# Attention on one core: the product with the inverse sums on GpSimd, row maxima six tiles ahead, and layer 2's maximum products on two groups of 64 rows

## Chip, core and metric

One Trainium2 chip, one of its cores. The time is that of the whole program on the device, in microseconds (us). The kernel before is measured in three runs, and one further execution is profiled.

## What is computed

The input is an image of 32 x 32 positions with 384 channels, that is 1024 tokens. Three residual blocks follow each other:

```
x = x + conv_attention(groupnorm(x))            # layer 1: 12 heads of 32, relative position terms
t = t + attention(layernorm(t))                 # layer 2: 12 heads of 32
t = t + experts(layernorm(t))                   # 8 experts, the best 2 of each token

per head:  attn = softmax(q k^T * scale (+ rel_h + rel_w in layer 1));  out = attn v
```

The change concerns the 12 heads of both attention layers.

## The kernel before, in words

Every engine has its own instruction stream, written out by hand, and semaphores tie them together. Each stream runs layer 1 (L = 0 in the code) and layer 2 (L = 1) with the same code. A layer first makes q, k and v, splits q and k into a rounded part and a rest, and writes them to DRAM by head; then come 12 heads, numbered 0 to 11; then the projection and the next normalisation. Heads 0, 1, 10 and 11 are written out, heads 2 to 9 are two turns of a loop of four heads.

A head is worked through in eight tiles of 128 keys, s = 0 to 7 (`head` in each engine's block):

- TensorE makes the transposed scores of tile s (`scores`, L618, and L620 for the position terms in layer 1), 128 keys by 1024 queries in two banks. Behind them it makes the *maximum products* (`max_scores`, L603): one tile of 128 queries against all 1024 keys, in two halves of 512 keys, from the head's own copies qm and km. After each odd s it makes the output products of two earlier tiles (`out_product`, L628). Only VectorE's maximum of each query is wanted from the maximum products.
- VectorE takes the maximum over each half of 512 (`maximum`, L891). The halves rotate through three PSUM banks (`RING`), so a product waits until VectorE has read the bank that was used three halves before. When the eight tiles of a head are done, the maxima are transposed (`turn_max`, L608), copied by ScalarE (`turned_max`), stored to DRAM and loaded as row 96 of qa (`place_max`), so that the scores of that head come out with the maximum subtracted.
- `AHEAD` says how many tiles the maximum products run ahead of the scores: with 5, tile s of head h makes tile s + 5 of head h + 1, or, from s = 3, tile s - 3 of head h + 2. The list `MAXIMA` holds this as (heads ahead, tile).
- ScalarE takes the exponential of each tile into one of six buffers of prob (L1074). GpSimd adds up tiles 0 to 5 in layer 1 and 0 to 4 in layer 2 (`add_tiles`, L514 for the first, L518 for the others, one 128x1024 addition each), and TensorE sums the remaining tiles and this sum over the keys (`sums`).
- Output products and sums of head h - 1 are finished at s = 1 of head h. ScalarE copies them to vsb (`keep_output`, L1100). At s = 3 to 6 VectorE inverts the sums in four pieces (`invert_sums`, L901) and after s = 6 multiplies (`output`, L906, 128x256), which counts o_ok up.
- SyncE issues the DMAs in one queue. One turn of its loop, for head h, is: `load_m(h + 1)` (qm and km, L379 and L380), `load_a(h)` (qa, ka, qb), in layer 2 three stores of zeros (L449), and `store(h - 2)`, which waits for o_ok and then issues four DMAs (L314). `load_m(h + 1)` waits for the end of the maximum products of head h - 1, whose buffers it overwrites, and stands behind the stores of head h - 3. TensorE waits for it (ld_m) before tile 0 of the maximum products of head h + 1.

In layer 1 qm and km have 96 rows in use: three parts of q and k of 32 rows. In layer 2 the product has 32 rows that count; rows 32 to 95 of qm are set to zero between the layers (L933), so that the same 96-row product can be used.

## Time and profile before

| | us |
|---|---|
| median of three runs | 1006.41 |
| lowest, highest | 1001.41, 1008.95 |
| the profiled execution | 1002.1 |
| its span in the trace | 1000.3 |
| layer 1's heads 2 to 9 | about 159 to 302 |
| layer 2's heads 2 to 9 | about 449 to 585 |
| experts | about 650 to the end |

The trace holds one execution. A row of a time line gives the start of a group of instructions, the time from the start of the first to the end of the last, the engine, the line of the kernel, the operation with output and inputs, the shapes, and in brackets how long the engine stood idle before it and who released it. A matmul's end is modelled and reaches into the next one, so the distance between starts is what counts on TensorE (PE). DVE is VectorE, ACT ScalarE, POOL GpSimd, SP SyncE; SPq is SyncE's queue of DMA issues.

### The profile page before, as it was taken

The numbers are of one execution on the slowest core, as the hardware profiler recorded it, in microseconds if no ns is written. First come the engines' busy times: TensorE is split into PE (matmuls) and PEld (weight loads), VectorE is DVE, ScalarE is ACT, GpSimd is POOL, SyncE is SP. The second block draws the span as 40 slices with busy tenths as digits, with TensorE's granted clock in tenths as the row PEclk, the third lists the DMA queues.
The fourth block names the chain that finished last, engine by engine and source line by source line (L and its number), as shares of the span: only waits on it lengthen the run. The fifth ranks groups of instructions, "written<-read, shape, count | busy, mean of one in ns | idle before, by whom it ended". The sixth has DMA issues, their size and how long they took to land.

```text
span 1000.3 us, 17750 instructions
## 1 busy us (share of the span) xinstructions
PE 879.1 (88%) x6029; PEld 641.9 (64%) x6030; DVE 526.9 (53%) x883; ACT 328.3 (33%) x582; POOL 457.2 (46%) x360
## 2 busy tenths in 40 slices
PE   4969899999998899999898978616999999999991
PEld 3457466566665444555454534516999999999991
DVE  4334767676776444878788772722233333233224
ACT  0212144554545222445454544201222322322230
POOL 0000076676778200346464665558076177077303
PEclk9989699999999999999999989957999999999996
DMA  9564723534424019335464571351356455455214
GB/s 291 109 147 150 271 76 87 130 104 110 127 84 154 11 32 231 92 84 176 127 206 126 195 241 37 125 185 49 115 179 219 145 174 197 167 181 176 87 32 141
DMA packets 74367, 139.23 MB, mean 139 GB/s; under 512 B 11000, under 2 KB 49080, under 8 KB 74320
## 3 DMA queue, kind: packets, MB, share of 16 engines
q1 hardware_dynamic: 62720, 120.42, 39.3%
q10 hardware_dynamic: 9552, 11.93, 3.6%
q0 software_dynamic: 2048, 6.29, 2.0%
q8 instruction: 24, 0.39, 0.2%
q14 instruction: 23, 0.19, 0.1%
HBM read 91.39 MB, written 43.55 MB: 135 GB/s over the span
## 4 chain that ended last, share of the span: by engine, by line
PE 43%; issue 8%; DVE 8%; POOL 6%; DMA 3%; ACT 1%; DVEq 0%; SPq 0%; POOLq 0%; ACTq 0%
PE ps L796 14%; PE ps L807 11%; DVE mhalf L891 4%; PE ps L628 4%; PE ps L585 3%; PE ps L603 3%; POOL qf L518 3%; PE ps L727 2%; PE ps L618 2%; POOL xs L547 1%; POOL gy L556 1%; PE ps L683 1%; DVE rec L901 1%; PE ps L778 1%; ACT prob L1074 1%
## 5 line engine op out<-in xcount | busy, mean ns | idle before, releaser
L891 DVE TENSOR_REDUCE mhalf<-ps 128x1 f32<-128x512 f32 x384 | 242.0, 679 | 95.6 <-PE ps L603 94.1
L1074 ACT ACTIVATE prob<-ps 128x1024 f32<-128x1024 f32 x192 | 190.5, 1026 | 186.7 <-PE ps L628 110.0
L518 POOL TENSOR_TENSOR qf<-qf,prob 128x1024 f32<-128x1024 f32 x84 | 206.1, 2453 | 18.2 <-POOL qf L518 8.1
L796 PE MATMUL ps<-xT,w 128*128 128x128 f32 x1440 | 166.8, 278 | 1.6 <-ACT xT L1146 1.4
L796 PEld LDWEIGHTS ps<-xT,w 128*128 128x128 f32 x1440 | 166.1, 194 | 2.1 <-issue 2.1
L603 PE MATMUL ps<-km,qm 96*128 96x512 f32 x384 | 145.3, 445 | 20.1 <-DVE mhalf L891 15.3
L618 PE MATMUL ps<-qa,ka 97*128 97x512 f32 x384 | 147.4, 426 | 8.6 <-DMA qa<-row 8.2
L1163 ACT ACTIVATE h_f<-ps,b1c 128x128 f32<-128x128 f32 x240 | 68.4, 368 | 215.6 <-PE ps L796 161.0
L603 PEld LDWEIGHTS ps<-km,qm 96*128 96x128 f32 x384 | 74.1, 194 | 71.5 <-DVE mhalf L891 51.9
L514 POOL TENSOR_TENSOR qf<-prob 128x1024 f32<-128x1024 f32 x24 | 57.1, 2379 | 134.7 <-ACT prob L1074 134.7
L628 PE MATMUL ps<-prob,va 128*32 128x256 f32 x1536 | 109.8, 393 | 0.0
L1018 DVE CAST h_hi<-h_f 128x512 fp32r<-128x512 f32 x60 | 33.6, 560 | 144.6 <-ACT h_f L1163 142.4
L499 POOL TENSOR_SCALAR w_hi<-w_raw 128x384 fp32r<-128x384 f32 x96 | 54.6, 569 | 112.1 <-DMA w_raw<-in_w 105.4
L501 POOL TENSOR_TENSOR w_lo<-w_raw,w_hi 128x384 fp32r<-128x384 f32 x96 | 101.2, 1054 | 8.0
L618 PEld LDWEIGHTS ps<-qa,ka 97*128 97x128 f32 x384 | 69.4, 192 | 50.7 <-ACT prob L1074 23.6
L528 POOL COPY va<-vf 128x256 f32 (+1 forms) x24 | 9.5, 396 | 187.7 <-DVE vf L877 102.4
L807 PE MATMUL ps<-w_hi,h_hi 128*128 128x384 f32 x240 | 82.0, 342 | 0.0
L807 PE MATMUL ps<-w_lo,h_hi 128*128 128x384 f32 x240 | 80.4, 335 | 0.0
L807 PE MATMUL ps<-w_hi,h_lo 128*128 128x384 f32 x240 | 80.4, 335 | 0.0
L620 PE MATMUL ps<-qb,eb 128*128 128x512 f32 x192 | 76.9, 400 | 0.0
L628 PEld LDWEIGHTS ps<-prob,va 128*32 128x32 f32 x1536 | 40.9, 111 | 47.3 <-issue 29.2
L585 PE MATMUL ps<-xnT,wqkv 128*128 128x512 f32 x144 | 63.6, 604 | 3.1 <-DVE xnT L852 3.1
(130 smaller groups left out, 874.5 us busy)
## 6 DMA issues: line engine op xcount, KB each, us to landing
w<-in_w SPq DMA_DIRECT2D x24, 768.0 KB, 7.4
w_raw<-in_w SPq DMA_DIRECT2D x24, 768.0 KB, 12.0
heads<-parts SPq DMA_DIRECT2D x56, 256.0 KB, 4.7
qa<-heads SPq DMA_DIRECT2D x24, 256.0 KB, 3.7
ka<-heads SPq DMA_DIRECT2D x24, 256.0 KB, 3.9
qb<-heads SPq DMA_DIRECT2D x12, 512.0 KB, 5.1
xs<-zero SPq DMA_DIRECT2D x8, 768.0 KB, 4.9
qm<-heads SPq DMA_DIRECT2D x12, 384.0 KB, 3.7
```

Source lines behind the costliest of these rows:

```text
L501: pool.tensor_tensor(w2_lo[b][:, c, :], w2_raw[b][:, c, :], f(w2_hi[b][:, c, :]), ALU.subtract).then_inc(w2_ok[b], 1)
L518: pool.tensor_tensor(acc[b], acc[b], prob[:, n % NP, :], ALU.add).then_inc(a_ok[L], 1)
L585: last = mm(ps[:, 2 * (u % 2) + half, :], wqkv[:, k, col * P:(col + 1) * P], xnT[:, k, half * HALF:(half + 1) * HALF], start=(k == 0), sto ...
L603: mm(max_bank(qt, half), qm[b][0:96, qt * P:(qt + 1) * P], km[b][0:96, half * HALF:(half + 1) * HALF], start=True, stop=True).then_inc(sm_ ...
L618: last = mm(out, ka[b][0:97, s * P:(s + 1) * P], qa[b][0:97, cols], start=True, stop=(L == 1))
L620: last = mm(out, eb[:, s * P:(s + 1) * P], qb[b][:, cols], start=False, stop=True)
L628: last = mm(ps[HD * r:HD * (r + 1), 6, half * QUARTER:(half + 1) * QUARTER], lhs, src[:, r * QUARTER:(r + 1) * QUARTER], start=start, stop ...
L796: last = mm(ps[:, g, c % HG * P:(c % HG + 1) * P], w1[b][:, k, c * P:(c + 1) * P], xT[:, k, :], start=(k == 0), stop=(k == KT - 1))
L807: last = mm(ps[:, 6, 0:C], h[:, c, :], w[:, c, :], start=(c == 0 and n == 0), stop=(c == HC - 1 and n == 2))
L891: v.tensor_reduce(mhalf[:, b, qt, half:half + 1], max_bank(qt, half), AX.X, ALU.max).then_inc(mx_ok[L], 1)
L1074: act.activation(prob[:, s % NP, :], ps[:, 2 + 2 * (s % 2):4 + 2 * (s % 2), :].rearrange("p a b -> p (a b)"), ACT.Exp).then_inc(p_ok[L], 1)
L1163: last = act.activation(h_f[:, c, :], ps[:, g, c % HG * P:(c % HG + 1) * P], ACT.Relu, bias=b1c[b][:, c:c + 1])
```

## The change

The product of the outputs with the inverse sums moves from VectorE to GpSimd, behind the last addition of the head after. `AHEAD` is 6 instead of 5. In layer 2 the first half of the keys is multiplied on rows 0 to 63 of the array and the second half on rows 64 to 127: qm and km grow to 128 rows, q's rounded part is loaded a second time into rows 64 to 95 of qm and the second half of k's into the same rows of km, and rows 96 to 127 are set to zero at the very start of VectorE's stream. The zeroing between the layers shrinks to rows 32 to 63.

```diff
-AHEAD = 5
+AHEAD = 6
-MAXIMA_FIRST = [[(1, 5)], [(1, 6)], [(1, 7)], [(2, 0)], [(2, 1)], [(2, 2)], [(2, 3)], [(2, 4)]]
+MAXIMA_FIRST = [[(1, 5), (1, 6)], [(1, 7)], [(2, 0)], [(2, 1)], [(2, 2)], [(2, 3)], [(2, 4)], [(2, 5)]]
-        qm = [put(f"qm{i}", [96, N], F32R) for i in range(2)]
-        km = [put(f"km{i}", [96, N], F32R) for i in range(2)]
+        qm = [put(f"qm{i}", [P, N], F32R) for i in range(2)]
+        km = [put(f"km{i}", [P, N], F32R) for i in range(2)]
@@ sync, load_m
                     sp.dma_start(f(km[b][0:HD, :]), rows(h, "K_HI")).then_inc(ld_m[L][b], 16)
+                    if L == 1:
+                        sp.dma_start(f(qm[b][64:96, :]), rows(h, "Q_HI")).then_inc(ld_m[L][b], 16)
+                        sp.dma_start(f(km[b][64:96, HALF:N]), rows(h, "K_HI")[:, HALF:N]).then_inc(ld_m[L][b], 16)
@@ gpsimd
-                def add_tiles(h, b, last=False):
+                def output(h, b):
+                    pool.wait_ge(o_rc[L], 4 * (h + 1))
+                    wait(pool, st_o[L][b], 32 * (h - b))
+                    pool.sem_inc(pool_in, 1)
+                    pool.tensor_tensor(osb[b][:], vsb[:, 0, :], rec[:], ALU.mult).then_inc(o_ok[L], 1)
+
+                def add_tiles(h, b, first=False, last=False):
                     for n in range(1, ADDS[L] + 1):
...
+                        if n == ADDS[L] and not first:
+                            output(h - 1, 1 - b)
+                    if last:
+                        output(h, b)
@@ tensor
-                n_m, n_a = (2, 5) if L == 0 else (2, 4)
+                n_m, n_a = (2, 5) if L == 0 else (4, 4)
...
-                        mm(max_bank(qt, half), qm[b][0:96, qt * P:(qt + 1) * P],
-                           km[b][0:96, half * HALF:(half + 1) * HALF], start=True, stop=True).then_inc(sm_ok[L], 1)
+                        rows = slice(0, 96) if L == 0 else slice(64 * half, 64 * half + 64)
+                        mm(max_bank(qt, half), qm[b][rows, qt * P:(qt + 1) * P],
+                           km[b][rows, half * HALF:(half + 1) * HALF], start=True, stop=True).then_inc(sm_ok[L], 1)
...
-                                pe.wait_ge(wide_ok, 4)
+                                pe.wait_ge(wide_ok, 6)
@@ vector, at its start
                 v.memset(f(ka[i][96:104, :]), 1.0)
+                for wide in (qm, km):
+                    v.memset(f(wide[i][96:P, :]), 0.0).then_inc(wide_ok, 1)
@@ vector, in the heads
-                def output(h, b):
-                    wait(v, st_o[L][b], 32 * (h - b))
-                    v.wait_ge(o_rc[L], 4 * (h + 1))
-                    v.tensor_tensor(osb[b][:], vsb[:, 0, :], rec[:], ALU.mult).then_inc(o_ok[L], 1)
...
-                        if s == 6 and not first:
-                            output(h - 1, 1 - b)
...
-                        for rows in (slice(32, 64), slice(64, 96)):
-                            v.memset(f(qm[i][rows, :]), 0.0).then_inc(wide_ok, 1)
+                        v.memset(f(qm[i][32:64, :]), 0.0).then_inc(wide_ok, 1)
...
-                output(NH - 1, 1)
```

The lines of the changed kernel are some steps further down: L511 is the product on GpSimd, L523 and L527 the additions, L617 the maximum products, L622 the transposition, L632 and L634 the scores, L642 the output products.

On GpSimd, in the loop of layer 1, the last addition of one head and what follows it. Before (qf holds the running sum, va the values, prob the exponentials):

```order
L518 TENSOR_TENSOR qf<-qf,prob 128x1024
L508 ISA
L514 TENSOR_TENSOR qf<-prob 128x1024
L284 ISA
L528 ISA
L528 COPY va_67<-vf 128x256
```

and now:

```order
L527 TENSOR_TENSOR qf<-qf,prob 128x1024
L508 REGISTER_ALU
L284 REGISTER_ALU
L511 TENSOR_TENSOR osb_72<-vsb,rec 128x256
L517 ISA
L523 TENSOR_TENSOR qf<-prob 128x1024
```

The product to osb has come between the last addition of a head and the first of the next.

On TensorE, in the loop of layer 1, tiles 2 and 3 of a head before (km_63 and qm_61 belong to the next head, km_64 and qm_62 to the one after it; qa, ka, qb are of the head itself):

```order
L618 MATMUL ps<-qa_58,ka_60 128x512
L620 MATMUL ps<-qb_66,eb 128x512
L602 REGISTER_ALU
L603 MATMUL ps<-km_63,qm_61 128x512
L602 REGISTER_ALU
L603 MATMUL ps<-km_63,qm_61 128x512
L284 REGISTER_ALU
L618 MATMUL ps<-qa_58,ka_60 128x512
L620 MATMUL ps<-qb_66,eb 128x512
L618 MATMUL ps<-qa_58,ka_60 128x512
L620 MATMUL ps<-qb_66,eb 128x512
```

and tile 2 now:

```order
L632 MATMUL ps<-qa_58,ka_60 128x512
L634 MATMUL ps<-qb_66,eb 128x512
L632 MATMUL ps<-qa_58,ka_60 128x512
L634 MATMUL ps<-qb_66,eb 128x512
L284 ISA
L617 MATMUL ps<-km_64,qm_62 128x512 x2
L622 MATMUL ps<-ident,mcol 8x128
L284 REGISTER_ALU
```

The first maximum products of the second head ahead stood behind tile 3 and stand behind tile 2, and the transposition directly behind them.

In SyncE's queue, in the loop of layer 2, the last of the four stores of an output and the loads behind it. Before:

```order
L314 DMA xnT<-osb_71 32x256
L284 REGISTER_ALU
L379 ISA
L379 DMA qm_61<-heads 32x1024
L380 ISA
L380 DMA km_63<-heads 32x1024
L284 REGISTER_ALU
```

and now:

```order
L314 DMA xnT<-osb_72 32x256
L284 REGISTER_ALU
L379 ISA
L379 DMA qm_62<-heads 32x1024
L380 ISA
L380 DMA km_64<-heads 32x1024
L382 DMA qm_62<-heads 32x1024
L383 ISA
L383 DMA km_64<-heads 32x512
L284 REGISTER_ALU
```

Two loads have been added; their place behind the stores is the same.

## Rows read from the trace of the kernel before

**Rows 1.** Busy time of each engine in a stretch of each layer: PE, PEld, DVE, ACT, POOL, clock.

```profile
250.00:300.00 50.00, 50.00 (x387) 31.99 (x389) 37.71 (x66) 24.04 (x27) 36.65 (x18) 1.00 0.38 106
550.00:600.00 50.00, 41.60 (x357) 22.02 (x353) 39.33 (x53) 24.65 (x30) 32.62 (x15) 0.94 0.65 217
```

**Rows 2.** TensorE's maximum products in the time line, layer 1.

```profile
198.29 0.73 PE L603 MATMUL ps<-km,qm 96*128 96x512 f32 x2 [0.26 <-DVE mhalf L891]
...
249.69 0.63 PE L603 MATMUL ps<-km,qm 96*128 96x512 f32 x2
...
251.09 0.88 PE L603 MATMUL ps<-km,qm 96*128 96x512 f32 x2
```

**Rows 3.** VectorE's products with the inverse sums in the time line, layer 1.

```profile
188.42 2.20 DVE L906 TENSOR_TENSOR osb<-vsb,rec 128x256 f32<-128x256 f32 x1
...
242.60 0.55 DVE L906 TENSOR_TENSOR osb<-vsb,rec 128x256 f32<-128x256 f32 x1
```

**Rows 4.** GpSimd's additions in the time line, layer 1.

```profile
159.46 2.39 POOL L514 TENSOR_TENSOR qf<-prob 128x1024 f32<-128x1024 f32 x1 [4.52 <-ACT prob L1074]
...
231.96 2.37 POOL L514 TENSOR_TENSOR qf<-prob 128x1024 f32<-128x1024 f32 x1 [4.25 <-ACT prob L1074]
...
243.05 2.38 POOL L518 TENSOR_TENSOR qf<-qf,prob 128x1024 f32<-128x1024 f32 x1 [0.18 <-ACT prob L1074]
249.69 2.39 POOL L514 TENSOR_TENSOR qf<-prob 128x1024 f32<-128x1024 f32 x1 [4.27 <-ACT prob L1074]
...
302.41 2.38 POOL L514 TENSOR_TENSOR qf<-prob 128x1024 f32<-128x1024 f32 x1 [4.19 <-ACT prob L1074]
```

**Rows 5.** TensorE in the time line, layer 2.

```profile
528.80 0.50 PE L603 MATMUL ps<-km,qm 96*128 96x512 f32 x1 [1.31 <-DVE mhalf L891]
...
533.28 0.62 PE L603 MATMUL ps<-km,qm 96*128 96x512 f32 x2
...
534.46 1.10 PE L603 MATMUL ps<-km,qm 96*128 96x512 f32 x2
...
540.71 0.63 PE L618 MATMUL ps<-qa,ka 97*128 97x512 f32 x2
541.17 0.76 PE L603 MATMUL ps<-km,qm 96*128 96x512 f32 x2
541.87 1.07 PE L628 MATMUL ps<-prob,va 128*32 128x256 f32 x16
```

**Rows 6.** VectorE's product with the inverse sums in the time line, layer 2.

```profile
525.69 2.45 DVE L906 TENSOR_TENSOR osb<-vsb,rec 128x256 f32<-128x256 f32 x1
```

**Rows 7.** SyncE's queue in the time line, layer 2: the loads of qm and km.

```profile
531.28 0.36 SPq L379 DMA_DIRECT2D qm<-heads  x1
531.84 0.35 SPq L380 DMA_DIRECT2D km<-heads  x1
```

**Rows 8.** GpSimd's additions in the time line, layer 2.

```profile
430.52 2.37 POOL L514 TENSOR_TENSOR qf<-prob 128x1024 f32<-128x1024 f32 x1 [4.85 <-ACT prob L1074]
...
448.63 2.37 POOL L514 TENSOR_TENSOR qf<-prob 128x1024 f32<-128x1024 f32 x1 [7.40 <-ACT prob L1074]
...
533.76 2.37 POOL L514 TENSOR_TENSOR qf<-prob 128x1024 f32<-128x1024 f32 x1 [5.90 <-ACT prob L1074]
...
542.19 2.38 POOL L518 TENSOR_TENSOR qf<-qf,prob 128x1024 f32<-128x1024 f32 x1 [0.18 <-POOL qf L518]
...
585.32 2.40 POOL L514 TENSOR_TENSOR qf<-prob 128x1024 f32<-128x1024 f32 x1 [5.91 <-ACT prob L1074]
```

**Rows 9.** Busy time and granted clock in a stretch of layer 2, columns as above.

```profile
442.00:450.00 8.00, 7.75 (x52) 3.96 (x52) 4.33 (x8) 3.75 (x5) 1.37 (x1) 0.79 0.49 139
```

**Rows 10.** TensorE at the start of layer 2's head 11, in the time line.

```profile
597.65 0.77 PE L618 MATMUL ps<-qa,ka 97*128 97x512 f32 x1 [5.49 <-DMA qa<-row]
```

**Rows 11.** VectorE at the program's start, in the time line.

```profile
2.74 0.91 DVE L824 MEMSET ka<- 8x1024 f32 x1 [0.16 <-issue]
...
4.23 1.36 DVE L838 BATCH_NORM_STATS2 stat<-xnT 128x6 f32<-128x512 f32 x2
```

More of the change, by code:

```diff
@@ L530, in _ @@
                 take_v(0, 0)
-                add_tiles(0, 0)
+                add_tiles(0, 0, first=True)
                 add_tiles(1, 1)
```

## The prediction

> **What bounds the kernel now.** I read four views in this order: the busy time by stretch, the time line of TensorE through one head of each layer, that of VectorE, SyncE's queue and GpSimd over the same stretch, and the sequence of heads seen from GpSimd's first addition. Call R the moment in a head at which TensorE comes to the maximum products of tile 2, M a pair of such products, S the scores of a tile.
>
> In layer 1 TensorE is busy for all of 50 us; in layer 2 for 41.6 of 50 [rows 1]. Layer 1's heads take (302.41 - 249.69) / 3 = 17.57 us where nothing disturbs them, and (302.41 - 159.46) / 8 = 17.87 over the loop [rows 4]. Layer 2's take (585.32 - 448.63) / 8 = 17.09 [rows 8]. So layer 1 has nothing to give on other engines, and layer 2 has some: in one head TensorE waits 1.31 us for VectorE, because VectorE's 256-column product took 2.45 us there [rows 5, 6]. In layer 1, where it fell into a gap of GpSimd's, the same product took 0.55 [rows 3].
>
> One loop counts above all. The loads of a head's qm and km stand in SyncE's queue behind the stores of an output made a head before, and M of the second head ahead waits for them. In layer 1 an output ends at 188.42 + 2.20 = 190.62 and M starts at 198.29, 7.67 later; another ends at 243.15, and M starts on time at 251.09, 7.94 later [rows 2, 3]. In layer 2 the output ends at 525.69 + 2.45 = 528.14, the loads of qm and km are issued at 531.28 and 531.84, and M starts at 534.46 [rows 5 to 7]; VectorE frees its bank at the same moment, so the row alone doesn't say which of the two it waited for. Load and slot meet within a few tenths in both layers: there is no slack for what comes later.
>
> **The change, part by part.**
>
> *The product on GpSimd.* It now stands behind the last addition. In layer 1 the additions run from 231.96 to 243.05 + 2.38 = 245.43, 13.47 us [rows 4]. The product has a quarter of the columns of an addition: 2.38 / 4 = 0.6, with a start gap of 0.2 some 0.8. It ends at R + 14.3 (the first addition starts at R: both at 249.69 [rows 2, 4]), where VectorE was done at 243.15, so 3.1 us later. In layer 2 the additions take 542.19 - 533.76 + 2.38 = 10.8 and start 0.48 behind R (533.28) [rows 5, 8]; with 0.87 the output ends at R + 12.15.
>
> *Maxima six ahead.* The first M of the second head ahead moves from tile 3 to tile 2: its slot is 251.09 - 249.69 = 1.4 us earlier in layer 1, 534.46 - 533.28 = 1.2 in layer 2.
>
> *Two more loads in layer 2.* They are issued 0.56 apart as the two before (531.28, 531.84 [rows 7]); with the gap to the next issue 0.6 each, 1.2 more before the last lands.
>
> *The loop, layer 1.* Output at R + 14.3, landing and weight load 7.8 later: M is possible at R + 22.1. TensorE comes to it at R + 17.3 (the 17.57 without the 0.25 by which the second M at 251.09 is slow, 0.88 against 0.63 [rows 2]). A wait X moves R of the next head but not the additions of its own head, so two waits in a row add up to 22.1 - 17.3 = 4.8, and a head takes (22.1 + 17.3) / 2 = 19.7. A first wait of 4.8 also holds the third and fourth additions (scores of tile 3 come late) by some 1.8 once. Eight heads (loads 4 to 11 stand behind a store): 8 x 19.7 + 2.4 (the first wait above the mean) = 160, against 142.95. **Plus 17.0 us.**
>
> *Layer 2's pairs.* If the two products run at once, each of the 8 pairs saves one start distance, 0.46 / 2 = 0.23 (S to M, 540.71 to 541.17 [rows 5]): 1.86 a head. But M now stands between products of 97 rows. The one change of array shape that the trace shows, M to the output products (541.17 to 541.87), costs 0.70 - 0.46 = 0.24 beyond the pair [rows 5]. A head gets 12 more changes of shape (three per two tiles). Bounds for one: nothing and 0.24, together 0 to 2.9 us a head; below nothing it can't be, since nothing is removed. I take 0.1, 1.2 a head, somewhat below the middle: the 0.24 also holds the weight loads of four column groups, which a change of row groups does not have.
>
> The Trainium skill speaks against this part: its page "TensorEngine Tiling (Array Packing)", section "Key Properties", says that changing the tiling mode, not only the tile, drains TensorE. The trace agrees for column groups, by the 0.24 above; no row here shows it for row groups. By the rule the upper bound holds, and the pairs would cost 1.0 a head instead of saving 0.7.
>
> *TensorE's own head in layer 2*, free of waits: 16.7 less 1.31, less 0.34 (1.10 against 0.76 for the pair at 534.46) and some 0.7 in smaller slips is 14.4 [rows 5]. Then - 1.86 + 1.2 + 0.45 (VectorE's 16 maxima and 4 reciprocals still fill their tiles) = 14.2. VectorE loses 2.4 a head and no longer binds.
>
> *The loop, layer 2.* M possible at R + 12.15 + 6.3 (528.14 to 534.46) + 1.2 = R + 19.7; period (19.7 + 14.2) / 2 = 17.0, eight times, with 2.8 for the first wait: 138.8 against 136.69. **Plus 2.1.** So what the pairs and the freed VectorE bring is spent waiting for the loads.
>
> *Head 1 of layer 2* has no load behind a store ahead of it. It took 448.63 - 430.5 = 18.1, part of it at a granted clock of 0.79 on average [rows 8, 9]; now 14.2 and a little: **minus 3.5.** *Head 10 to 11*: TensorE waits 5.49 for the row of maxima [rows 10]; the transposition now stands a tile and a pair of output products earlier, 1.9 us: **minus 1.9.**
>
> *The clock.* In 442 to 450 the granted clock averages 0.79, its lower level of 1.2 GHz for part of the stretch, after such a wait [rows 9]; the same view shows it in three of the loop's eight heads. Waits of 3 us a head should bring more of it. A fall costs some 1.5, half of which the load's lateness hides: **plus 2** (bounds 0 and 6).
>
> *Start.* Four more memsets of 32x1024 run ahead of the first statistics, which begin the moment VectorE is free. A memset of 1024 columns takes 0.91 and a start gap of 0.16 (2.74), 1.07 together, and nothing stands between the last memset and the statistics at 4.23 [rows 11]: four are **plus 4.3**, less only if x lands after 4.23. Two memsets less between the layers lie beside TensorE's head 10 and bring nothing.
>
> *Ends of the layers.* The last product waits for reciprocals on another engine and takes 0.6 instead of 0.43: 0.5 each, and 0.8 once in layer 1, where GpSimd's additions are the end: **plus 1.8.**
>
> **Sum:** 4.3 + 17.0 + 1.8 - 3.5 + 2.1 - 1.9 + 2 = 21.8. The profiled execution took 1002.1 (span 1000.3), so 1023.9, say **1024 us**. That execution lies 4.3 below the median of the three runs (1006.41); against that median it would be 1.8% slower. About 1% is what a measurement of this kernel can tell from no change.
>
> **The rivals.**
>
> *A, forecast:* M waits for the load in both layers. For it: load and slot already meet. Against it: no row of layer 1 shows a wait of this size, only its beginning.
>
> *B, the loads keep up, faster.* The place is the same M. It decides at the point where the last load lands before the slot, that is, if from R to landing is under 17.3 in layer 1 and 14.2 in layer 2 instead of 22.1 and 19.7. Then layer 1 gives 8 x 0.57 = 4.6, layer 2 8 x 2.9 = 23.1, head 1 3.5, head 10 1.9, against 6.1 for start and ends: 1002.1 - 27.0 = 975. For it: layer 2's real waits of 1.31. Against it: the 7.67 and 6.32 measured between an output and its M.
>
> *C, changes of shape cost the upper bound.* TensorE's head in layer 2 is 15.9, the period 17.8: 8 x 17.8 + 1.9 for the first wait is plus 7.6 instead of 2.1; head 1 gives 1.9; the clock falls in every head, plus 6: 1002.1 + 4.3 + 17.0 + 1.8 + 7.6 - 1.9 - 1.9 + 6 = 1035. (This is also what the skill's rule on tiling modes comes to here.)
>
> *D, the pairs are free and the clock holds.* TensorE's head in layer 2 is 14.4 - 1.8 = 12.6, the period 16.15, with 3.6 for the first wait 132.8, minus 3.9; head 1 minus 5.1: 1002.1 + 4.3 + 17.0 + 1.8 - 3.9 - 5.1 - 1.9 = 1014, within 1% of the median.
>
> *E, the pairs don't overlap* (one starts behind the other): 1.86 back on TensorE, of which the loop shows half, 7.4 in eight heads, and 1.9 in head 1: 1033. It has its chance inside A and C.
>
> **How the numbers follow.** A 0.60, C 0.15, D 0.16, B 0.09. The range reaches from below D (1015, less if x lands late and hides the memsets: 4.3, and if layer 1's waits are 0.5 shorter each: 4) to C: 1006 to 1038. Faster by over 1% is most of B, 0.08; within 1% is D and a rest, 0.17; slower 0.75.
>
> **What would show it.** In the profile after, TensorE's largest wait is M for km or qm, 2 to 5 us in heads 2 to 9 of both layers, and GpSimd's first additions of layer 1 follow each other by 19.7 (17.57 before); the output ends 0.8 behind the last addition; SyncE's stores wait for GpSimd. The two products of a layer 2 pair start within a few ns of each other; S behind them starts 0.1 later than before. The first matmul of TensorE moves from 9.35 us by 4.3. The forecast is wrong if M starts without waiting at tile 2, if layer 2's period is under 16, or if the first statistics don't move.

## The result, and the profile after

The changed kernel takes 1067.69 us (median of four runs, 1059.92 to 1075.65), the kernel before, on the same chip, 1004.78 (1001.41 to 1008.95). The ratio is 1.0625, 95% interval 1.0524 to 1.0725: slower by 6%. The prediction said 1024, range 1006 to 1038. The direction and the place were right, the size was 44 us short. The profiled execution took 1059.9, its span is 1058.1 against 1000.3, and the mean granted clock of TensorE 0.917 against 0.945.

In this part R is the start of GpSimd's first addition in a head (L523, before L514). The prediction's R, the moment at which TensorE comes to the maximum products of tile 2, lies a few tenths beside it; where a forecast counts from that moment, I count from it too and say so. The 24 first additions divide the span:

| stretch | before | after | difference | forecast |
|---|---|---|---|---|
| to R of head 0, layer 1 | 123.7 | 129.8 | +6.1 | +4.3 |
| heads 0 and 1 | 35.7 | 39.8 | +4.1 | 0 |
| heads 2 to 9 | 143.0 | 162.5 | +19.5 | +17.0 |
| head 10 | 16.1 | 16.8 | +0.7 | 0 |
| R of head 11 to R of head 0, layer 2 | 96.4 | 100.8 | +4.4 | +1.3 |
| head 0 | 15.6 | 18.4 | +2.8 | 0 |
| head 1 | 18.1 | 16.8 | -1.3 | -3.5 |
| heads 2 to 9 | 136.7 | 158.0 | +21.3 | +2.1 |
| head 10 | 18.3 | 15.8 | -2.5 | -1.9 |
| from R of head 11 to the end | 396.6 | 399.3 | +2.7 | +0.5 |
| clock, in no one place | | | | +2 |

The list of waits of the changed kernel has at the place of the forecast (engine, output and line waited for, releaser, then us in all, times, longest):

```profile
PE ps L617 <- DMA km<-heads: 32.5, 19, 2.9
POOL osb L511 <- DVE rec L917: 22.6, 9, 4.5
```

Before, the first of these was 2.2 us in 4 waits, and the second did not exist. The busy time by stretch, in the columns of [rows 1]: two of the same stretches, then the eight heads of either loop.

```profile
250.00:300.00 50.00, 44.82 (x321) 27.18 (x314) 27.05 (x47) 21.79 (x27) 33.39 (x18) 0.93 0.41 116
550.00:600.00 50.00, 47.07 (x337) 20.79 (x337) 32.69 (x57) 22.40 (x25) 29.24 (x17) 0.86 0.49 157
170.00:332.00 162.00, 147.73 (x1096) 91.86 (x1097) 96.08 (x168) 70.10 (x80) 103.39 (x56) 0.96 0.34 95
485.00:643.00 158.00, 142.49 (x1034) 64.21 (x1035) 96.00 (x168) 69.48 (x81) 84.60 (x48) 0.86 0.48 150
```

TensorE, never idle in 250 to 300 before, is now idle for 5.2 us of it. In layer 2 it looks busier than before (47.07 against 41.60), but at a clock of 0.86: the same products last longer. Read without its clock, the busy share would have said that TensorE waits less there than before.

One turn of the loop in layer 1, GpSimd and then TensorE, answers to [rows 2 to 4]:

```profile
188.42 2.34 POOL L523 TENSOR_TENSOR qf<-prob 128x1024 f32<-128x1024 f32 x1 [4.67 <-ACT prob L1081]
...
202.20 0.73 POOL L511 TENSOR_TENSOR osb<-vsb,rec 128x256 f32<-128x256 f32 x1
208.94 2.34 POOL L523 TENSOR_TENSOR qf<-prob 128x1024 f32<-128x1024 f32 x1 [6.01 <-ACT prob L1081]
```

```profile
188.18 0.39 PE L634 MATMUL ps<-qb,eb 128*128 128x512 f32 x1
191.28 0.73 PE L617 MATMUL ps<-km,qm 96*128 96x512 f32 x2 [2.71 <-DMA km<-heads]
...
211.16 0.72 PE L617 MATMUL ps<-km,qm 96*128 96x512 f32 x2 [2.07 <-DMA km<-heads]
```

TensorE comes to the maximum products of tile 2 at 191.28 - 2.71 = 188.57. The output ends at 202.93, 14.4 later (forecast 14.3), and the M that needs the load behind it starts at 211.16, after a wait of 2.07: 22.6 later (forecast 22.1).

The same turn in layer 2, to be read against [rows 5, 7, 8]: TensorE, then GpSimd, then SyncE's queue.

```profile
527.45 0.61 PE L617 MATMUL ps<-km,qm 64*128 64x512 f32 x2 [1.80 <-DMA km<-heads]
...
548.69 0.50 PE L617 MATMUL ps<-km,qm 64*128 64x512 f32 x2 [1.75 <-DMA km<-heads]
...
563.83 0.73 PE L632 MATMUL ps<-qa,ka 97*128 97x512 f32 x2
566.68 0.49 PE L617 MATMUL ps<-km,qm 64*128 64x512 f32 x2 [2.12 <-DMA km<-heads]
```

```profile
540.89 0.73 POOL L511 TENSOR_TENSOR osb<-vsb,rec 128x256 f32<-128x256 f32 x1 [3.80 <-DVE rec L917]
547.25 2.35 POOL L523 TENSOR_TENSOR qf<-prob 128x1024 f32<-128x1024 f32 x1 [5.63 <-ACT prob L1081]
...
558.51 0.73 POOL L511 TENSOR_TENSOR osb<-vsb,rec 128x256 f32<-128x256 f32 x1 [0.49 <-DVE rec L917]
564.94 2.35 POOL L523 TENSOR_TENSOR qf<-prob 128x1024 f32<-128x1024 f32 x1 [5.70 <-ACT prob L1081]
```

```profile
559.38 2.60 SPq L314 DMA_DIRECT2D xnT<-osb  x4
562.79 0.37 SPq L379 DMA_DIRECT2D qm<-heads  x1
563.37 0.35 SPq L380 DMA_DIRECT2D km<-heads  x1
563.81 0.37 SPq L382 DMA_DIRECT2D qm<-heads  x1
564.36 0.32 SPq L383 DMA_DIRECT2D km<-heads  x1
```

The chain can be followed in them. TensorE comes to the maximum products of tile 2 at 548.69 - 1.75 = 546.94; the output ends at 559.24, 12.3 later (forecast 12.15); then come four stores, four loads, and M at 566.68, 19.7 later (forecast 19.7). What the forecast has not is the moment at which TensorE comes to that M: 566.68 - 2.12 = 564.56, which is 15.9 behind the M of a head before (548.69); the sum took TensorE's own head at 14.2.

The clock, for the head that holds this turn and the one before it, then for pieces of the earlier one:

```profile
525.95:547.25 21.30, 19.49 (x129) 8.62 (x129) 12.07 (x21) 8.73 (x11) 10.56 (x6) 0.76 0.47 140
547.25:564.94 17.69, 15.66 (x129) 7.31 (x129) 11.91 (x21) 8.84 (x11) 10.62 (x6) 1.00 0.52 165
```

```profile
526.00:530.00 4.00, 2.55 (x7) 1.26 (x7) 1.31 (x3) 2.09 (x4) 3.47 (x3) 0.71 0.82 168
530.00:534.00 4.00, 4.00 (x22) 1.50 (x21) 1.74 (x4) 1.01 (x2) 3.82 (x2) 0.50 1.04 386
534.00:538.00 4.00, 4.00 (x21) 1.64 (x22) 3.49 (x6) 1.40 (x2) 2.49 (x2) 0.51 0.16 60
538.00:542.00 4.00, 4.00 (x34) 1.87 (x33) 2.88 (x5) 2.04 (x2) 0.73 (x1) 1.00 0.00 0
```

Both heads issue 129 products and wait about as long for the load (1.80 at 527.45, 1.75 at 548.69). After the first of these waits the clock stood at its lower level of 1.2 GHz (0.50) until about 538, and that head took 3.6 us more. Five of layer 2's eight loop heads have a granted clock under 1.00, and three of layer 1's. Of layer 2's other three, two take 17.7; the third, behind the longest head (23.53), takes 16.15 and so gives a part back. Layer 1's other five take 18.7 to 20.5, mean 19.5. An estimate of the clock's part from these heads is 158.0 - 8 x 17.7 = 16.4 and 162.5 - 8 x 19.5 = 6.5, together 23 us in the two loops. Head 0 of layer 2 is 2.8 longer at a granted clock of 0.83, which makes about 26 us where the sum has 2; but e4 below, where nothing waits for these loads, has the same head 0 (18.45 at 0.83), so its 2.8 don't come from the loop.

### The profile page after: what moved, and what is told of

Same layout as the page of the kernel before. It is cut to its first block, busy times and chain, and to the rows that moved or that the text cites. A ratio compares the mean times of both kernels' runs of the same rounds, so it can differ in the third digit from the quotient of the medians.

```text
span 1058.1 us, 17804 instructions
## 1 busy us (share of the span) xinstructions
PE 914.5 (86%) x6029; PEld 638.3 (60%) x6030; DVE 492.2 (47%) x861; ACT 331.3 (31%) x582; POOL 473.6 (45%) x384
## 4 chain that ended last, share of the span: by engine, by line
PE 57%; issue 11%; POOL 10%; DMA 8%; DVE 6%; SPq 5%; ACT 2%; POOLq 0%; ACTq 0%; DVEq 0%
PE ps L810 13%; PE ps L821 10%; PE ps L617 6%; PE ps L642 6%; PE ps L598 6%; PE ps L632 6%; POOL qf L527 6%; DMA km<-heads 5%; SPq L314 3%; PE ps L634 2%; PE ps L741 2%; PE ps L697 2%; DVE mhalf L907 2%; PE ps L719 2%; ACT prob L1081 2%
## 5 line engine op out<-in xcount | busy, mean ns | idle before, releaser
L1081 ACT ACTIVATE prob<-ps 128x1024 f32<-128x1024 f32 x192 | 193.6, 1026 | 227.1 <-PE ps L642 100.3
L527 POOL TENSOR_TENSOR qf<-qf,prob 128x1024 f32<-128x1024 f32 x84 | 202.4, 2410 | 27.1 <-ACT prob L1081 12.8
L632 PE MATMUL ps<-qa,ka 97*128 97x512 f32 x384 | 162.7, 467 | 7.3 <-ACT prob L1081 4.2
L617 PE MATMUL ps<-km,qm 96*128 96x512 f32 (+1 forms) x384 | 135.3, 502 | 38.2 <-DMA km<-heads 32.5
L810 PEld LDWEIGHTS ps<-xT,w 128*128 128x128 f32 x1440 | 165.3, 194 | 2.1 <-issue 2.1
L617 PEld LDWEIGHTS ps<-km,qm 96*128 96x128 f32 (+1 forms) x384 | 65.9, 203 | 105.9 <-issue 60.8
L523 POOL TENSOR_TENSOR qf<-prob 128x1024 f32<-128x1024 f32 x24 | 56.6, 2357 | 142.2 <-ACT prob L1081 142.2
L642 PE MATMUL ps<-prob,va 128*32 128x256 f32 x1536 | 119.8, 423 | 0.0
L632 PEld LDWEIGHTS ps<-qa,ka 97*128 97x128 f32 x384 | 69.9, 203 | 70.8 <-issue 35.2
L541 POOL COPY va<-vf 128x256 f32 (+1 forms) x24 | 12.5, 519 | 192.2 <-DVE vf L893 107.4
L634 PE MATMUL ps<-qb,eb 128*128 128x512 f32 x192 | 78.2, 407 | 0.0
L642 PEld LDWEIGHTS ps<-prob,va 128*32 128x32 f32 x1536 | 42.9, 116 | 52.7 <-issue 34.7
L917 DVE RECIPROCAL rec<-vsb 128x64 f32<-128x64 f32 x96 | 49.8, 534 | 44.5 <-ACT vsb L1107 44.5
```

The source lines that it names most:

```text
L527: pool.tensor_tensor(acc[b], acc[b], prob[:, n % NP, :], ALU.add).then_inc(a_ok[L], 1)
L617: mm(max_bank(qt, half), qm[b][rows, qt * P:(qt + 1) * P], km[b][rows, half * HALF:(half + 1) * HALF], start=True, stop=True).then_inc(sm_ ...
L632: last = mm(out, ka[b][0:97, s * P:(s + 1) * P], qa[b][0:97, cols], start=True, stop=(L == 1))
L634: last = mm(out, eb[:, s * P:(s + 1) * P], qb[b][:, cols], start=False, stop=True)
L642: last = mm(ps[HD * r:HD * (r + 1), 6, half * QUARTER:(half + 1) * QUARTER], lhs, src[:, r * QUARTER:(r + 1) * QUARTER], start=start, stop ...
L810: last = mm(ps[:, g, c % HG * P:(c % HG + 1) * P], w1[b][:, k, c * P:(c + 1) * P], xT[:, k, :], start=(k == 0), stop=(k == KT - 1))
```

## The experiments

"Before" in each group is the kernel before, run on the same chip in turn with the experiments: medians 1002.21 (e1 to e4), 1002.97 (e5 to e8), 1003.94 (g1 to g4) and 1006.21 (h2). R2 to R10 is the loop of heads 2 to 9; "km waits" is the first row of the list of waits.

### The three parts alone: e1_ahead, e2_gpsimd, e3_rows

e1 is the kernel before with the two lines of constants (`AHEAD` 6 and its list), e2 with the product on GpSimd, e3 with the two row groups, their loads and memsets.

> The kernel before with AHEAD = 6 alone. Theory 1 (the loads of qm and km, queued behind the stores of an output, arrive late): the slot of the first maximum product is 1.4 us earlier in layer 1 and 1.2 in layer 2, the loads are not, so TensorE waits in heads 2 to 9 of both layers; period 19.1 instead of 17.9 in layer 1 (plus 10), 17.9 instead of 17.1 in layer 2 (plus 6), and lower clock after the waits, plus 20 in all. Rival (the change of array shape in layer 2 is the cost): nothing changes, within 3 us of before.

> The kernel before with the product of the outputs on GpSimd alone. Theory 1: the output ends 3.1 us later in layer 1 and 0.5 in layer 2; plus 13 in layer 1, minus 3 in layer 2 (VectorE is freed of 2.4 us a head), plus 10 in all. Rival (shape of the array): 5 to 15 us faster, since only VectorE loses work.

> The kernel before with the two groups of 64 rows alone (with its two more loads and the four memsets at the start). Theory 1: start plus 4.3; layer 1 unchanged; in layer 2 the last load lands 1.2 later, and TensorE's own head is 0.7 longer: period 18.3 instead of 17.1, plus 10; plus 16 in all, 20 with a lower clock. Rival (the 64-row products lower the clock and drain the array by themselves): layer 2 alone is 20 or more longer, and little of it stands as a wait for km.

| | us | ratio (interval) | R2 to R10, layer 1 | layer 2 | km waits |
|---|---|---|---|---|---|
| e1 | 1033.74 | 1.0287 (1.0223 to 1.0351) | 162.0 | 140.4 | 21.3 in 18 |
| e2 | 1015.73 | 1.0105 (1.0063 to 1.0146) | 157.2 | 129.8 | 21.3 in 14 |
| e3 | 1011.31 | 1.0073 (1.0044 to 1.0102) | 144.8 | 133.6 | 7.6 in 11 |

Each part alone costs time: 31.5, 13.5 and 9.1, together 54 of the 63 of the whole change. An earlier slot (e1) and a later output (e2) each open the wait, as the loop of the prediction says. e1 costs 31.5 where I expected 20, by itself more than the prediction gave to the whole change; e2 costs 13.5 where I expected 10. The rivals of e1 (no change) and of e2 (faster) are out. e3 cost half of what I expected and made layer 2's loop 3 us shorter; its loss is at the start (+4.3) and in the stage in which layer 2's first maximum products run among the projections (24.9 against 23.0). In e2 layer 2 is 7 us shorter: there VectorE's product really was in the way [rows 6], and its going is worth more than the 9.3 us that this loop now waits for km.

### The cause taken away: e4_after_loads_first, e5_before_loads_first

```diff
@@ sync, ahead of the loop
                 load_m(2, 0)
+                load_m(3, 1)
                 load_a(2, 0)
-                load_m(3, 1)
-                store(0, 0, 0)
@@ sync, a turn of the loop
                         load_m(h + 1, n % 2)
+                        store(h - 3, n % 2, n, q)
                         load_a(h, 1 - n % 2)
...
-                        store(h - 2, 1 - n % 2, n + 1, q)
```

> The changed kernel, with SyncE's queue in another order: the loads of qm and km stand ahead of the stores of an output instead of behind them, one head earlier. Theory 1: the waits for km are gone, the period is 17.4 in layer 1 and 15.3 in layer 2, the granted clock is above 0.95, and the whole is some 10 us faster than the kernel before (start plus 4.3, ends plus 2, layer 1 minus 2, layer 2 minus 15). Rival (shape of the array, its clock): still 20 or more slower than before, with layer 2's period above 18.

> The kernel before with only SyncE's queue reordered (loads of qm and km ahead of the stores of an output). Theory 1 (before the change load and slot met with nothing to spare, but nearly without waits): layer 1 minus 2 (the head of 19.5 becomes 17.6), layer 2 minus 1 to 3, VectorE's 2.4 us product stays the wait of a layer 2 head; 2 to 5 us faster in all. Rival (the order of the queue is a gain of its own): 10 or more faster.

e4, the changed kernel with only this order changed, takes 1002.89, ratio to before 1.0003 (0.9967 to 1.0038). Its loops are 140.6 and 126.5, both at a granted clock of 1.00, and the list of waits has left:

```profile
PE ps L617 <- DMA km<-heads: 0.5, 1, 0.5
```

So nearly the whole loss hangs on the order of stores and loads in SyncE's queue. I had expected 10 us less than before. The two loops give 12.6, but the stretch to R of head 0 takes 6.0 more than before, the stage between the layers 5.8, head 0 of layer 2 2.9 and the end 3.2; and layer 2's head is 15.8 where I expected 15.3. The same edit to the kernel before (e5) gives 1000.41, ratio 0.997 (0.9934 to 1.0006): as good as nothing, since there the loads were just in time.

### What the parts are worth once nothing waits: e6, e7, e8, g4

e6_loads_ahead_gpsimd is e4 without the row groups, e7_loads_gpsimd also with `AHEAD` 5; e8_loads_late_memset is e4 with the four memsets moved behind the first normalisation; g4_one_group is e4 with both halves on one group:

```diff
-                        rows = slice(0, 96) if L == 0 else slice(64 * half, 64 * half + 64)
+                        rows = slice(0, 96) if L == 0 else slice(0, 64)
```

> The changed kernel with the loads first and without the two groups of 64 rows (96 rows as before, two loads, no memsets at the start). Theory 1 (row groups cost 0.7 us a head, the memsets 4.3 and the stage of the values 1.9): 12 to 14 us faster than the same kernel with row groups, about 990, layer 2's period 15.1. Rival (the row groups do save their 1.9 us a head once the loads are in time): slower than with them in layer 2, period 17, total gain under 5.

> The kernel before with the loads first and the product on GpSimd, maxima five tiles ahead as before. Theory 1: as with six ahead, 988 to 992, since with the loads in time the sixth tile buys only the earlier transposition before head 11 (2 us). Rival (six ahead is what frees VectorE's waits at tile 2 and 3): 5 or more slower than with six.

> The changed kernel with the loads first, all its parts kept, and the four memsets of rows 96 to 127 moved from VectorE's start to behind the first normalisation, where VectorE waits 6.5 us for ScalarE. Theory 1: the first statistics go back to 4.2 us and the whole gets 4.3 us faster than with the memsets at the start, 998. Rival (x lands late anyway): no difference.

> The changed kernel with the loads of qm and km ahead of the stores (as e4), but in layer 2 both products of a pair on rows 0 to 63, so that they can't run at once; the rows hold the same numbers, so the computation is the same. Theory: in e4 the second product of a pair starts 0.05 to 0.25 us behind the first, so it overlaps it only in part; here it starts 0.23 behind, S behind a pair comes up to 0.2 later and layer 2's head grows by 0.4 to 1.6 us (15.8 to 16.2 to 17.4), the time by 4 to 15 us over e4's 1003. Rival (the groups don't overlap at all or the overlap is eaten by the wait for VectorE's bank): same as e4 within 2 us.

| | us | ratio (interval) | layer 2, a head |
|---|---|---|---|
| e6 | 987.07 | 0.9838 (0.979 to 0.9886) | 15.05 |
| e7 | 988.91 | 0.9852 (0.9804 to 0.99) | 15.35 |
| e8 | 999.91 | 0.997 (0.994 to 0.9999) | 15.8 |
| e4 | 1002.89 | 1.0003 (0.9967 to 1.0038) | 15.8 |
| g4 | 1020.42 | 1.0158 (1.0085 to 1.0231) | 16.63 |

e6 beats both kernels, by a little more than expected. e7 takes the same time within the intervals, as expected: once the loads are in time the sixth tile brings nothing clear. The freed VectorE does: from e5 to e7, whose only difference is the product on GpSimd, it is 11.5 us or 1.2%. In e8 the first statistics start at 4.41 instead of 8.55, and R of head 0 of layer 1 comes 3.7 earlier than in e4. The medians differ by 3.0 with overlapping intervals, so that the spans (996.5 and 1000.8) differ by just the expected 4.3 is partly luck. g4 is 17.5 over e4 by the medians, more than the expected 4 to 15, and 9.5 by the profiled executions; its head in layer 2 grows by 0.8, inside the expected 0.4 to 1.6. The time lines of TensorE in layer 2 give the prices of row groups; 96 rows (e6) first, then two groups (e4), then one group of 64 (g4):

```profile
531.44 0.63 PE L613 MATMUL ps<-km,qm 96*128 96x512 f32 x2
531.90 0.63 PE L628 MATMUL ps<-qa,ka 97*128 97x512 f32 x2
532.37 0.75 PE L613 MATMUL ps<-km,qm 96*128 96x512 f32 x2
533.05 1.07 PE L638 MATMUL ps<-prob,va 128*32 128x256 f32 x16
```

```profile
530.29 0.50 PE L617 MATMUL ps<-km,qm 64*128 64x512 f32 x2
530.72 0.73 PE L632 MATMUL ps<-qa,ka 97*128 97x512 f32 x2
531.39 0.69 PE L617 MATMUL ps<-km,qm 64*128 64x512 f32 x2
532.00 1.07 PE L642 MATMUL ps<-prob,va 128*32 128x256 f32 x16
```

```profile
531.89 0.73 PE L617 MATMUL ps<-km,qm 64*128 64x512 f32 x2
532.56 0.74 PE L632 MATMUL ps<-qa,ka 97*128 97x512 f32 x2
533.22 0.73 PE L617 MATMUL ps<-km,qm 64*128 64x512 f32 x2
533.88 1.07 PE L642 MATMUL ps<-prob,va 128*32 128x256 f32 x16
```

From M to S it is 0.46, 0.43 and 0.67 us; from S to M 0.47, 0.67 and 0.66; from M to the output products 0.68, 0.61 and 0.66. g4 against e6 is the mixing of shapes without overlap: 0.2 more from pair to pair in each direction between 97 rows and 64. The rows don't show in which instruction the 0.2 arises, for the distances inside a pair grow too: g4's second product of the pair at 531.89 starts at 532.23, 0.34 behind the first, where e6's is 0.23 behind. e4 against g4 is the overlap: 0.24 where the pair stands ahead of S (its two products end within 0.50), 0.05 where it stands ahead of output products (0.69).

The second value is not the array's. The two products can only run together if both their banks are free, and a narrower view of the pair at 531.39 shows that the second starts 0.18 late, 0.05 after VectorE has finished reading the half whose bank it takes:

```profile
530.83 0.69 DVE L907 TENSOR_REDUCE mhalf<-ps 128x1 f32<-128x512 f32 x1
531.57 0.50 PE L617 MATMUL ps<-km,qm 64*128 64x512 f32 x1
```

The product waits by the code until this read is done. Every pair of e4's loop ahead of output products is late in this way, 24 by 0.19 and eight by 0.60; in the pairs ahead of S the two products start within 0.004 of each other. So what g4's rival says of VectorE's bank is true of half the pairs.

The heads agree in sign, with less than the rows would give: 1.6 a head for the shapes (16.63 - 15.05) where twelve changes of 0.2 would be 2.4, and 0.8 for the overlap (16.63 - 15.81) where four times 0.24 and four times 0.05 would be 1.2. The overlap is real and costs more than it brings. The Trainium skill's page "TensorEngine Tiling (Array Packing)", section "Key Properties", says that a change of tiling mode drains the engine. These 0.2 us are in line with it for row groups, where the trace of before could show only column groups; the drain itself is in no row.

### The clock and the late output: g1_fill, g2_ahead_gpsimd, g3_early_inverse, h2_fill_early

g1 gives TensorE something to do during the wait, g3 moves VectorE's reciprocals; h2 has both; g2 is the two parts of the change without row groups.

```diff
@@ g1, tensor, ahead of max_scores' wait for the load
+                    if qt == 0 and not (isinstance(h, int) and h < 2):
+                        pe.wait_ge(mx_ok[L], 2 * TT * h - 1)
+                        for _ in range(8):
+                            mm(max_bank(0, 0), ka[b][0:97, 0:P], qa[b][0:97, 0:HALF], start=True, stop=True)
@@ g3, vector
-                        if 3 <= s < 7 and not first:
-                            invert_sums(h - 1, s - 3)
+                        if 2 <= s < 6 and not first:
+                            invert_sums(h - 1, s - 2)
```

> The changed kernel, but TensorE makes 8 extra products of 97 rows and 512 columns (about 1.9 us) ahead of each wait for the loads of qm and km in heads 2 to 11; their result is overwritten by the maximum product behind them. Theory 'clock': the waits of 3 us let the granted clock fall and that fall is the larger part of what my sum missed. With TensorE fed during the wait, the mean granted clock rises from 0.917 to 0.94 or more, layer 2's heads become steady at about 17.7 us and layer 1's at about 19.2 to 19.5, and the time is 10 to 25 us shorter than the changed kernel's 1067.7 although work was added. Rival 'waits alone': the clock only follows the waits and costs little; then the extra products lie inside the wait and the time is that of the changed kernel within 6 us, or longer.

> The changed kernel, with VectorE's four pieces of the inverse sums one tile earlier (behind tiles 2 to 5 instead of 3 to 6). Theory: in layer 2 GpSimd's product waits for VectorE's last reciprocal, which stands behind the maxima of tile 6 that the late load has delayed; with the reciprocals a tile earlier the product follows the last addition, the undisturbed head of layer 2 falls from 17.7 to about 17 and the time by 5 to 15 us; layer 1 (output ends by GpSimd's additions) stays. Rival (what the prediction said: the output ends by GpSimd's additions in both layers): no change within 3 us.

> Maxima six ahead and the product on GpSimd, without the row groups, loads behind the stores as before. By the theory of the loop the two parts add: each alone took 31.5 and 13.4 us more than before, so together 1045 to 1052, km waits in both layers; the row groups' own share (start 4.3, values stage 1.9, two more loads, changes of shape) is then the remaining 12 to 20 us to the changed kernel. Rival: the row groups are what makes the loop of layer 2 bite (two more loads and the shape changes); then this kernel takes under 1040.

> The changed kernel with both edits at once: 8 extra products of 97 rows ahead of the wait for the loads (as g1_fill), and the inverse sums one tile earlier (as g3_early_inverse). Theory: the prediction's sum failed at two terms, the clock (2 us) and layer 2's loop (period 17.0 by a two-head loop whose output ends with the additions). With both causes taken away, layer 1's heads take 19.6 to 20.0 at a granted clock of 1.00 (the sum said 19.7) and layer 2's 17.0 to 17.5 at 1.00 (the sum said 17.0), and the time is 15 to 30 us under the changed kernel's 1067.7, below both single edits (1052.7 and 1058.2). Rival (the two edits take away the same thing, the clock's fall, and not two): the time is that of g1_fill within 4 us, with layer 2's undisturbed heads still at 17.6.

| | us | ratio (interval) | R2 to R10, layer 1 | layer 2 | clock in the two |
|---|---|---|---|---|---|
| after | 1067.69 | 1.0625 (1.0524 to 1.0725) | 162.5 | 158.0 | 0.96, 0.86 |
| g1 | 1052.74 | 1.0445 (1.0361 to 1.0529) | 158.2 | 153.0 | 1.00, 0.92 |
| g2 | 1044.07 | 1.0378 (1.0287 to 1.0468) | 165.3 | 151.0 | 0.95, 0.85 |
| g3 | 1058.19 | 1.054 (1.0461 to 1.062) | 166.9 | 149.0 | 0.94, 0.90 |
| h2 | 1050.41 | 1.0447 (1.0396 to 1.0499) | 158.2 | 141.3 | 1.00, 1.00 |

*g1* gives TensorE 15 to 16 us more work in each loop, and its median is 15 us lower, as the clock theory expected. The intervals of the two ratios just touch (1.0524 and 1.0529), and g1's profiled execution is its slowest (1061.24), so g1 alone would not carry this; h2, whose interval ends at 1.0499, does. The busy time of h2, which has the same filling and lost the clock nowhere in the loops, columns as above:

```profile
172.00:330.00 158.00, 156.63 (x1161) 101.03 (x1161) 96.12 (x168) 70.55 (x80) 104.02 (x57) 1.00 0.37 100
485.00:626.00 141.00, 139.11 (x1096) 69.88 (x1094) 94.64 (x168) 69.31 (x80) 84.93 (x48) 1.00 0.54 168
```

More products (1096 against 1034), no fall, and layer 2's loop is 16.7 us shorter than the changed kernel's. Layer 1's is 4.3 shorter (158.2 in both g1 and h2). Extra products can only add work, so these 21 us are a check on the chip of the 23 estimated from the undisturbed heads; h2 also has the reciprocals moved, but g1's heads at 1.00 in layer 2 take the same 17.6 to 17.9. The expectation that g1's profiled clock reaches 0.94 failed for that execution (0.927, heads of 22.84 and 24.10 in layer 2 at 0.78 and 0.72, after waits of 1.49 and 0.80); two of its other three runs had 0.940 and 0.944.

*g3* fits its expectation in the loop, 149.0 against 158.0, and its span is 7 shorter; GpSimd's wait for the reciprocals falls from 22.6 to 7.1 us. Layer 1's loop, expected to stay, is 4.4 longer, at 0.94. The two intervals of the ratio overlap, so the whole time alone would not carry it. Its two heads at 1.00 that stand behind no slowed head take 17.60 and 17.15, not much under 17.7; those behind a slowed one take 15.8. What the move helps are heads in which the clock fell: there, in the changed kernel, the output waits for the reciprocals (3.80 at 540.89 above) and ends at 541.62, R + 15.7 instead of R + 12.0, so a late head hands its lateness to the next load. In the undisturbed head the same wait is 0.49.

*h2* doesn't tell its two theories apart. Its heads of layer 2 are at 17.6 as the rival said, but TensorE is busy for 139 of 141 us: the filling itself sets the head, 15.8 + 1.8. My expectation of 17.0 to 17.5 had left the filling out. Its time and g1's are the same, also as the rival said. For the same reason the 19.8 of g1 and h2 in layer 1 is no proof of the forecast 19.7; the changed kernel's own undisturbed heads (19.5) and g2's (19.99, 20.00, 19.56, 19.31) are.

*g2* is where the parts should add up: 31.5 + 13.5 = 45 expected, 40.1 measured. Row groups cost the other 23 us in the changed kernel, more than the 12 to 20 that I expected, and 9 alone.

## Why the prediction was wrong

Right: that the loads of qm and km bound both loops, the chain from R (the prediction's) to output, stores, loads and M (22.6 and 19.7, forecast 22.1 and 19.7), layer 1's head of 19.7 (18.7 to 20.5 without falls, mean 19.5), the 4.3 of the memsets (statistics at 8.55 for 4.23), head 10 (-2.5 for -1.9). What the prediction found missing, a wait for the load in layer 1, the trace of before had once in small, 0.99 us in the one loop head of 19.5 us:

```profile
179.49 0.73 PE L603 MATMUL ps<-km,qm 96*128 96x512 f32 x2 [0.99 <-DMA km<-heads]
```

e4 shows the cause: without that order in the queue the loss is gone. Four terms failed.

1. *The clock, plus 2 with 6 as its bound.* It measured about 23 in the two loops (21 by h2) and 3 in head 0 of layer 2. The step "a fall costs some 1.5, half of which the load's lateness hides" failed twice. A fall costs 3.6 (21.30 against 17.69), in the longest head 5.8 (23.53), and in most heads it isn't hidden: it delays VectorE's reciprocals, the output, and so the next load. The number of falls was set by nothing but the word "more", and its base was misread: in the trace of before two of the loop's eight heads are under 1.00 (both 0.91), not three. The clock is 24 of the 36 us by which the profiled execution exceeds the sum.
2. *TensorE's own head in layer 2, 14.2.* It is 15.8 (e4), 1.6 more. 1.0 of that is the overlap: the pairs save 0.8 and not 1.86, mainly because VectorE's bank holds back half of them. 0.4 is the mixing of shapes, 1.6 a head where the sum had 1.2 (0.2 a change in the rows, where I chose 0.1 from 0 to 0.24). The rest is the head with 96 rows, 15.05 (e6) and not 14.4 + 0.45. So the net of the row groups is +0.76 a head, where the sum had -0.7. In the loop half of the 1.6 counts, (19.7 + 15.8) / 2 = 17.8 for 17.0, measured 17.7: eight heads without falls are 141.6 against the sum's 138.8. It also takes 1.6 of the -3.5 of head 1.
3. *Layer 1, head 1, 0.* Its loads stand behind no store, but behind the five DMAs of `load_a(2)`, and the slot that is a tile earlier meets them: a wait of 1.60 at 150.44 and a granted clock of 0.92, 20.99 us for 17.8. e4 puts them ahead of these DMAs as well and has 17.7.
4. *The stage between the layers.* The first maximum products of layer 2 change the shape there too: 1.9 us (24.9 for 23.0), the same in e3, e4 and the changed kernel, and in no term of the sum.

One term looks better than it was. Layer 1's loop measured +19.5 for +17.0, but 6.5 of it is the clock, so the waits alone brought 13: the closeness of the two numbers is luck in part. Some 7 us of the rest were not traced: 1.8 ahead of layer 1's heads, 0.9 in its head 0, 0.7 in its head 10, 1.2 more between the layers and 2.2 at the end.

Of the rivals, A was the mechanism. C had TensorE's head (15.9, measured 15.8) and the period (17.8, measured 17.7) of layer 2 right, but by luck: its shapes cost 2.9 and its pairs save 1.86, where 1.6 and 0.8 were measured; and it fell short by the clock. B, that the loads keep up, is the state of e4, made by another edit: there layer 1's loop gave 2.4 of its 4.6 us and layer 2's 10.2 of its 23.1, the head being 15.8 and not 14.2, so that 1003 came of 975; D is out; E is out by g4, since the pairs do overlap. That two products of a pair start together holds for those ahead of S only. The range was too narrow because its only entry for the clock was 0 to 6. What stays open: which wait is followed by a fall. Waits of 1.80 and 1.75 us in neighbouring heads differ in it, a head of layer 1 with a wait of 2.71 had none, and heads in g1 fell after waits of 1.49 and 0.80.

## What to carry to other kernels

Before work is moved to a later place or its slot to an earlier one, look at what stands behind it in the same DMA queue: here a store of one head held the load of another, the whole of a 6% loss went away with the stores moved behind the next loads, and with the loads in time the freed VectorE brought its 1.2%. A new wait on TensorE in a loop that was full is priced with the clock it loses and with who is late next, not by its own length. Two products on row groups overlap only if both find a free bank, and here the mixing of shapes cost twice what the overlap brought: count the changes and the banks first.

## What the runs showed of the hardware

- After a wait of 1.80 us the granted clock stood at 0.50 from about 530 to 538 in a head of layer 2, which took 21.30 us where its neighbour at 1.00 took 17.69. With extra products ahead of the waits and the reciprocals a tile earlier (h2) it stayed at 1.00 in both loops, and the kernel was faster by 17 us (1050.41 for 1067.69) in spite of 15 to 16 us more work in each loop; in g1 it stayed at 1.00 in layer 1's loop only (0.92 in layer 2's).
- Where pairs of 97-row and 64-row products alternate on one group (g4), the distance from pair to pair is 0.66 to 0.67 us in both directions, against 0.46 to 0.47 where they have 96 and 97 rows (e6).
- Two 64-row products of 512 columns on different row groups (e4) end within 0.50 us together, one after the other on the same group (g4) in 0.73.
- GpSimd's product of 128x256 took 0.73 us, on VectorE 2.45 in layer 2 and 0.55 in a gap of GpSimd's [rows 3, 6].
